# Attention in a fused Trainium2 kernel: bulk loads and the stores of x1 issued by ScalarE, and the inverse sums' way through memory as two items

## What is computed

```
q, k, v = split(x @ c_attn_w.T + b)              # 16 heads of 16
q_lat, k_lat, v_lat = q @ q2l, k @ kv2l, v @ kv2l  # 32 latents a head
q_lat, k_lat = rope(q_lat), rope(k_lat)
att = softmax(causal((q_lat @ wqk.T) @ k_lat.T * 32**-0.5))
y   = (att @ v_lat) @ l2o.T, heads joined, @ cproj.T
x1  = layernorm(x + y)
f   = layernorm(x1 + two_of_eight_experts(x1)) * g + b   # gate, top 2; w1, norm, gelu, w2
out = layernorm(x1 + f)
```

## Time and profile before

| | before |
|---|---|
| runs (us) | 2360.25, 2360.39, 2362.74; median 2360.39 |
| profiled execution: span | 2336.8 us; its total is not listed |
| attention phase, first x to the late items | about 27 to 1577 us of the span |
| expert and combining phases | about 1665 to 2337 us |
| TensorE / VectorE / ScalarE / GpSimd busy | 90% / 74% / 58% / 56% |
| granted TensorE clock, mean | 0.939 |
| SyncE's queue (q1) | 236.43 MB |
| ScalarE's queue (q10) | 9.44 MB |

### The profile page before, as it was taken

The page is one execution under the profiler, slowest core; times in us unless marked ns, Lnnn a source line. Parts: engine busy times, 40 slices in busy tenths (PEclk is TensorE's granted clock), DMA queues, the critical chain, the costliest instruction groups (busy, mean ns, idle before and its releaser), DMA issues. The chain is left out here.

```text
span 2336.8 us, 43530 instructions
## 1 busy us (share of the span) xinstructions
PE 2092.7 (90%) x12268; PEld 1464.7 (63%) x12268; DVE 1721.4 (74%) x4995; ACT 1365.5 (58%) x3316; POOL 1308.8 (56%) x1478
## 2 busy tenths in 40 slices
PE   4898999899899899899999999983399999999698
PEld 3554655555555555465556555642399999999587
DVE  3676687677678668668767767836488888888498
ACT  1265655655565565565555556563288887888454
POOL 2355464654764665666465476454577777777000
PEclk7899998999999999999889899995699999999899
DMA  6556556546565554655654556515122222222575
GB/s 176 127 135 142 118 115 149 126 106 150 127 135 128 135 122 118 156 118 116 149 123 109 140 124 146 115 39 213 26 74 74 76 75 76 74 74 69 182 243 168
DMA packets 190406, 284.46 MB, mean 122 GB/s; under 512 B 54072, under 2 KB 111056, under 8 KB 190032
## 3 DMA queue, kind: packets, MB, share of 16 engines
q1 hardware_dynamic: 168608, 236.43, 42.7%
q0 software_dynamic: 17152, 35.81, 5.0%
q10 hardware_dynamic: 4416, 9.44, 1.1%
HBM read 100.03 MB, written 37.90 MB: 59 GB/s over the span
## 5 line engine op out<-in xcount | busy, mean ns | idle before, releaser
L544 ACT ACTIVATE probs<-scores_T 128x512 f32<-128x512 f32 (+3 forms) x1536 | 654.4, 492 | 243.8 <-PE scores_T L433 240.7
L783 POOL TENSOR_SCALAR_AFFINE_SELECT probs<-probs 128x256 f32<-128x256 f32 x512 | 205.7, 410 | 522.4 <-ACT probs L544 519.4
L492 PE MATMUL ring<-k_stack,q_stack_b 96*128 96x512 f32 (+3 forms) x1024 | 396.3, 429 | 22.1 <-DVE neg_part L691 10.4
L691 DVE TENSOR_REDUCE neg_part<-ring 128x1 f32<-128x512 f32 x512 | 333.6, 685 | 97.6 <-PE ring L492 95.6
L433 PE MATMUL scores_T<-q_stack_b,k_stack 98*128 98x512 f32 (+3 forms) x1024 | 318.1, 387 | 45.4 <-ACT probs L544 44.5
L450 PE MATMUL o_ps<-probs,v_ones 128*17 128x512 f32 (+3 forms) x3072 | 341.8, 518 | 2.1 <-POOL probs L783 1.8
L492 PEld LDWEIGHTS ring<-k_stack,q_stack_b 96*128 96x128 f32 x1024 | 192.3, 196 | 227.4 <-issue 72.6
L696 DVE CUSTOM_DVE_ANT_0 ring<-ring,mask 128x384 f32<-128x384 f32 (+3 forms) x512 | 243.6, 508 | 113.5 <-PE ring L492 111.4
L696 DVE CUSTOM_DVE_ANT_0 ring<-ring,mask,neg_part 128x384 f32<-128x384 f32 (+3 forms) x512 | 260.5, 555 | 63.5 <-PE ring L492 63.3
L1107 ACT ACTIVATE o_sb<-ht_ps,ln_b,ln_g 128x128 f32<-128x128 f32 x544 | 217.9, 450 | 87.1 <-PE ht_ps L1056 86.6
L433 PEld LDWEIGHTS scores_T<-q_stack_b,k_stack 98*128 98x128 f32 x1024 | 186.3, 198 | 99.6 <-ACT probs L544 78.6
(11 more groups left out here) (190 smaller groups left out, 4552.8 us busy)
## 6 DMA issues: line engine op xcount, KB each, us to landing
u_rot<-u SPq DMA_DIRECT2D x128, 256.0 KB, 3.7
k_stack<-u_rot SPq DMA_DIRECT2D x128, 256.0 KB, 4.3
lat_w<-lat_split SPq DMA_DIRECT2D x32, 512.0 KB
q_stack_a<-u_rot SPq DMA_DIRECT2D x64, 256.0 KB
q_stack_b<-u_rot SPq DMA_DIRECT2D x64, 256.0 KB
k_stack<-u SPq DMA_DIRECT2D x64, 256.0 KB, 4.7
y<-y_rows SPq DMA_DIRECT2D x32, 512.0 KB, 6.7
x_raw<-in_xT SPq DMA_DIRECT2D x16, 512.0 KB, 5.3
```

Of the source, the lines that this page charges most:

```text
L492: nc.tensor.matmul(out[:, 0:k1 - k0], q_stack[qb // 4][0:3 * L, row_buf(n, qb // 4), h, P * (qb % 4):P * (qb % 4) + P], k_stack[0:3 * L, n ...
L544: nc.scalar.activation(probs[:, s % 2, h, cols], sc[(t + j) % 3][:, HALF - w:HALF], ACT.Exp).then_inc(exp_done, 1)
L691: nc.vector.tensor_reduce(neg_part[:, n % 2, part_col], src[:], AX_X, ALU.max, negate=True).then_inc(max_taken, 1)
L783: nc.gpsimd.affine_select(both, both, [[0, 2], [1, P]], ALU.is_ge, zero, base=0, channel_multiplier=-1).then_inc(kept, 1)
```

## The change

ScalarE's list now holds LAT, X, RES and the stores of x1 but the last one, and the loads and stores are issued there, with the waits they had (`bulk`). Every engine gets a list of its own from the same places plus a lag per engine and kind (`LAGS`); the only lag is -3.25 places for X on ScalarE. The places of X become (-58.75, 4.5), so that VectorE splits at 13.25 and 17.75 and ScalarE issues at 10 and 14.5. INV is cut into INV (7.25) and SPREAD (9.25), both SyncE's. A B item becomes two, one for each block, at the same place, so their order stays as it was.

```diff
--- before.py
+++ after.py
@@ -176,13 +176,16 @@
 
 
 PLACES = {
-    "LAT": (-53.5, 0), "Uq": (-50.25, 0.875), "SWAPq": (-49.25, 0), "ROPEq": (-45, 0), "WQ": (-41.5, 1.625),
+    "B": (0, 0),     "LAT": (-53.5, 0), "Uq": (-50.25, 0.875), "SWAPq": (-49.25, 0), "ROPEq": (-45, 0), "WQ": (-41.5, 1.625),
     "QL": (-41, 1.125), "STACKq": (-32.25, 0.875), "Uk": (-43.75, 0.625), "SWAPk": (-43, 0), "ROPEk": (-37.25, 0.5),
     "KH": (-34.75, 1.75), "KL": (-33.75, 1.875), "STACKk": (-29.75, 6.375), "S": (-27.75, 22.375), "MT": (-4.5, 0),
-    "MD": (-3.25, 0), "PV": (5.25, 2), "OE": (11.5, 15.625), "PACK": (24.75, 0), "RCP": (28.75, 0), "INV": (31.25, 0),
-    "Y": (36.5, 0), "X": (-60.75, 2.5), "V": (-23.5, 1.5), "RES": (4.5, 0), "ZB": (10.75, 0), "C": (39.5, 1),
+    "MD": (-3.25, 0), "PV": (5.25, 2), "OE": (11.5, 15.625), "PACK": (24.75, 0), "RCP": (28.75, 0), "INV": (31.25, 0), "SPREAD": (33.25, 0),
+    "Y": (36.5, 0), "X": (-58.75, 4.5), "V": (-23.5, 1.5), "RES": (4.5, 0), "ZB": (10.75, 0), "C": (39.5, 1),
     "NORM": (43.5, 0), "NX": (49.25, 0.75), "ZT": (53.5, 1.5), "G": (54.5, 1.5), "STORE": (68.25, 0),
     "R": (66.5, 0.375), "CNT": (72.25, 0.375), "SCAT": (77, 3.5)}
+
+
+LAGS = {"sync": {}, "tensor": {}, "scalar": {"X": -3.25}, "vector": {}, "gpsimd": {}}
 
 
 def attention_phase(nc, dram, wts, consts, xs, lat_dram, inv_dram, x1_dram, token_of_row, routes, tail, attention,
@@ -265,7 +268,7 @@
         def unit_items(n):
 
             b, g = n // GROUPS, n % GROUPS
-            at = [(HG * s + h, ("B", n, s, h)) for s in range(6) for h in range(HG)]
+            at = [(HG * s + h + j * PLACES["B"][1], ("B", n, s, h, j)) for s in range(6) for h in range(HG) for j in range(2)]
 
             def put(name, *items):
                 first, pace = PLACES[name]
@@ -290,6 +293,7 @@
             put("PACK", ("PACK", n))
             put("RCP", ("RCP", n))
             put("INV", ("INV", n))
+            put("SPREAD", ("SPREAD", n))
             if n % 2:
                 put("Y", ("Y", n))
             if g == 0 and b:
@@ -320,9 +324,16 @@
                     or it[0] in ("C", "NORM", "NX", "ZT", "G", "STORE", "R", "CNT", "SCAT") and it[1] == B - 1)
 
         R_STEPS, R_CHOSEN, R_COUNTED = 22, 12, 15
-        items = [it for _, it in sorted((p for n in range(UNITS) for p in unit_items(n)), key=lambda p: p[0])]
-        main, late = [it for it in items if not is_late(it)], [it for it in items if is_late(it)]
-        items = main + late
+        placed = [p for n in range(UNITS) for p in unit_items(n)]
+        late = [it for _, it in sorted(placed, key=lambda p: p[0]) if is_late(it)]
+
+        def order_of(engine):
+
+            lag = LAGS[engine]
+            return [it for _, it in sorted(placed, key=lambda p: p[0] + lag.get(p[1][0], 0)) if not is_late(it)]
+
+        main = {engine: order_of(engine) for engine in LAGS}
+        items = main["tensor"] + late
         RING = ("S", "U", "WQ", "MT", "C", "ZT", "G", "V", "CNT")
         ring_place = {it: i for i, it in enumerate(it for it in items if it[0] in RING)}
 
@@ -346,6 +357,26 @@
 
         ring_users = sorted(ring_place, key=lambda it: ring_place[it])
 
+        def bulk(engine, it):
+            kind, n = it[:2]
+            if kind == "LAT":
+                if n:
+                    engine.wait_ge(u_ready[1], 2 * n)
+                engine.dma_start(lat_w[:].bitcast(F32), lat_dram[n % GROUPS]).then_inc(lat_loaded, 16)
+            elif kind == "X":
+                kc = it[2]
+                if 2 * n + kc > KC:
+                    engine.wait_ge(x_lo_ready, 2 * n + kc - KC)
+                engine.dma_start(x_raw[:], dram["xT"][n, P * kc:P * kc + P, :]).then_inc(x_loaded, 16)
+            elif kind == "RES":
+                if n:
+                    engine.wait_ge(x1_stored, 16 * n)
+                    engine.wait_ge(logits_ready, TB * n)
+                engine.dma_start(z[:], dram["x"][n].rearrange("(tb p) c -> p tb c", p=P)).then_inc(res_loaded, 16)
+            elif kind == "STORE":
+                engine.wait_ge(x1_ready, TB * n + TB)
+                engine.dma_start(x1_dram[n].rearrange("(tb p) c -> p tb c", p=P), z[:]).then_inc(x1_stored, 16)
+
         def sync_items(sp, items):
             for it in items:
                 kind, n = it[:2]
@@ -353,15 +384,6 @@
                     for dst, name in ((rank, "rank"), (base, "base"), (before, "before"), (ones, "ones"),
                                       (ids_f, "ids_f")):
                         sp.dma_start(dst[:], dram[name]).then_inc(tables, 16)
-                elif kind == "LAT":
-                    if n:
-                        sp.wait_ge(u_ready[1], 2 * n)
-                    sp.dma_start(lat_w[:].bitcast(F32), lat_dram[n % GROUPS]).then_inc(lat_loaded, 16)
-                elif kind == "X":
-                    kc = it[2]
-                    if 2 * n + kc > KC:
-                        sp.wait_ge(x_lo_ready, 2 * n + kc - KC)
-                    sp.dma_start(x_raw[:], dram["xT"][n, P * kc:P * kc + P, :]).then_inc(x_loaded, 16)
                 elif kind == "SWAP":
                     s = it[2]
                     sp.wait_ge(u_ready[s], 2 * n + 2)
@@ -396,20 +418,15 @@
                 elif kind == "INV":
                     sp.wait_ge(inv_ready, n + 1)
                     sp.dma_start(inv_dram[n].rearrange("h (j i) -> (h j) i", i=L), inv[:]).then_inc(inv_kept, 16)
+                elif kind == "SPREAD":
                     sp.wait_ge(inv_kept, 16 * n + 16)
                     if n >= 2:
                         sp.wait_ge(y_ready, n // 2)
                     row = P // 2 * (n % 2)
                     sp.dma_start(inv_rep[row:row + P // 2, :],
                                  inv_dram[n].unsqueeze(1).to_broadcast([HG, HD, T])).then_inc(inv_spread, 16)
-                elif kind == "RES":
-                    if n:
-                        sp.wait_ge(x1_stored, 16 * n)
-                        sp.wait_ge(logits_ready, TB * n)
-                    sp.dma_start(z[:], dram["x"][n].rearrange("(tb p) c -> p tb c", p=P)).then_inc(res_loaded, 16)
-                elif kind == "STORE":
-                    sp.wait_ge(x1_ready, TB * n + TB)
-                    sp.dma_start(x1_dram[n].rearrange("(tb p) c -> p tb c", p=P), z[:]).then_inc(x1_stored, 16)
+                elif kind == "STORE" and n == B - 1:
+                    bulk(sp, it)
 
         def tensor_items(pe, items):
             for it in items:
@@ -420,19 +437,19 @@
                     if place >= 4:
                         pe.wait_ge(*freed(ring_users[place - 4]))
                 if kind == "B":
-                    s, h = it[2:]
-                    t = 2 * (24 * n + HG * s + h)
-                    if s == 0 and h == 0:
+                    s, h, j = it[2:]
+                    t = 2 * (24 * n + HG * s + h) + j
+                    if s == 0 and h == 0 and j == 0:
                         pe.wait_ge(max_row, 64 * n + 64)
                         if n == 0:
                             pe.wait_ge(consts_set, 3)
                     c, blocks = step_blocks(s)
-                    for j, (kb, q0, w, cols) in enumerate(blocks):
-                        if t + j >= 3:
-                            pe.wait_ge(exp_done, t + j - 2)
-                        nc.tensor.matmul(sc[(t + j) % 3][:, HALF - w:HALF], k_stack[:, n % 2, h, P * kb:P * kb + P],
-                                         q_stack[c][:, row_buf(n, c), h, q0 - HALF * c:q0 - HALF * c + w],
-                                         start=True, stop=True).then_inc(sc_full, 1)
+                    kb, q0, w, cols = blocks[j]
+                    if t >= 3:
+                        pe.wait_ge(exp_done, t - 2)
+                    nc.tensor.matmul(sc[t % 3][:, HALF - w:HALF], k_stack[:, n % 2, h, P * kb:P * kb + P],
+                                     q_stack[c][:, row_buf(n, c), h, q0 - HALF * c:q0 - HALF * c + w],
+                                     start=True, stop=True).then_inc(sc_full, 1)
                 elif kind == "PV":
                     s, j = it[2:]
                     b, g = n // GROUPS, n % GROUPS
@@ -534,15 +551,17 @@
                 if kind in RING:
                     place = ring_place[it]
                     src = ring[place % 4]
-                if kind == "B":
-                    s, h = it[2:]
-                    t = 2 * (24 * n + HG * s + h)
-                    if h == 0 and 6 * n + s >= 2:
+                if kind in ("LAT", "X", "RES") or kind == "STORE" and n < B - 1:
+                    bulk(act, it)
+                elif kind == "B":
+                    s, h, j = it[2:]
+                    t = 2 * (24 * n + HG * s + h) + j
+                    if h == 0 and j == 0 and 6 * n + s >= 2:
                         act.wait_ge(pv_done, 2 * (6 * n + s - 1))
-                    for j, (_, _, w, cols) in enumerate(step_blocks(s)[1]):
-                        act.wait_ge(sc_full, t + j + 1)
```

(22 more changed lines are left out.)

## The result

The kernel after takes **2379.59 us** (median of 9 runs, 2370.90 to 2386.96), beside 2360.25 for the kernel before in the same measurement (9 runs, 2351.24 to 2374.83). The ratio is **1.0071**, with an interval of 1.0044 to 1.0098: slower by 0.7%, where I forecast 0.3% faster. 2379.6 also lies above the range of 2334 to 2377. (Times here are medians over all runs of a kernel; the ratios leave out the few runs of before that a slower state of the chip disturbed.)

What follows compares the result with a forecast made beforehand. TensorE, busy 90% of the span, was taken as the bound through its standstills and half clock. Terms +3 + 2 + 5.6 - 14.0 - 2 - 1 = -6.4 us took 2360.4 to 2354 us; range 2334 to 2377.

Steps and rivals of the forecast that it cites:

- Who issues: SyncE's queue: losing 32 us of issues and sending q stacks sooner gains 0; bounds 0 and -9 us.
- First x: Early unit: VectorE's single 1.9 us wait for x goes away, -2 us; bounds 0 and -5.
- x's new places on VectorE: Splits at 13.25 and 17.75 don't fit before the transpose: +0.8 us in seven units, +5.6; bounds 0 and +16.
- the clock: TensorE in the six alike x units: all become the short 51.33 us kind, -14.0 us; bounds -25 and +14.
- ScalarE's issues: ScalarE carries 32 us of issues, 9% reaching TensorE: +3 us, or +8 if issues last 1.38 us; bounds 0 and +32.
- The wait moved to ScalarE: ScalarE, before x's second half: 1.2 us of wait less 0.9 idle, in seven units, +2 us; bounds 0 and +16.
- Latent weights later: Projection on TensorE: latent weights, issued later by ScalarE, still land in time, 0 us; bounds 0 and +24.
- Rival (c): Projection waits for latent weights if landing exceeds 4.3 us: +24 us, 2384 us; chance 0.12.
- The residual: GpSimd's 6.6 us of waits shrink as ScalarE issues the residual 1 or 2 us earlier: -1 us; bounds 0 and -6.6.
- The base: Whole kernel: profiled span 2336.8 us, with the median 23.6 us above it, left alone by the change.
- (b): Second split stops the transpose, half clock in all six x units: +14 and +3 us, 2377 us; chance 0.15.
- (a): Whole kernel: nothing moves, since SyncE had slack and ScalarE pays little; within 4 us of 2360; chance 0.25.

Runs made afterwards that it cites:

- experiment 9: Kernel after with all loads and stores issued by SyncE and x's splits at places 11.25 and 17.75: 2373.36 us, 1.0072 of before.
- experiment 7: Kernel after with only x on ScalarE (issues at 10 and 14.5); latent weights, residual and stores back on SyncE: 2374.88 us, 1.0046 of before.
- experiment 6: Kernel after with all loads and stores issued by SyncE, x at the new places (splits at 13.25 and 17.75): 2324.33 us, 0.9861 of before.
- experiment 12: Kernel after with everything issued by SyncE and x at its old places, only the cut items left: 2359.30 us, 0.9989 of before.
- experiment 10: Kernel after, all on SyncE, splits at 11.25 and 17.75, q stacks held until x's first half landed: 2350.19 us, 0.9971 of before.
- experiment 11: Kernel after with everything issued by SyncE and x's splits at places 13.25 and 15.75: 2338.54 us, 0.9920 of before.
- experiment 1: Kernel after with ScalarE issuing the first half of x at place 6.25 instead of 10: 2332.73 us, 0.9861 of before.
- experiment 5: Kernel after with x's first half issued at place 6.25 on ScalarE and the residual given back to SyncE: 2322.27 us, 0.9835 of before.
- experiment 8: Kernel after with only x on ScalarE, first half at place 6.25; latent weights, residual and stores on SyncE: 2323.07 us, 0.9856 of before.
- experiment 2: Kernel after with SyncE holding the q stacks in x units until x's first half is in: 2337.11 us, 0.9885 of before.

## Why the prediction was wrong

The order of issue against the clock of the unit explains the x units of all versions. Times are from the transfer of row maxima that opens the unit, each from one unit of the trace:

```
                          x issued   VectorE there   x landed    late by
before (from 1272.60)       24.3         31.7        by 31.7       -
all on SyncE, new places    24.1         35.2        by 35.2       -
experiment 9 (from 920.68)  24.1         31.7           34.4      2.7
after (from 914.27)         30.1         35.4           39.3      4.0
```

SyncE ran ahead of its list: with x at place 11.25 or 13.25 alike it issued the first half 24 us into the unit, as soon as the inverse sums had been spread. ScalarE, tied to its exps, reaches place 10 at 30 us. Beside the stacks the load takes 9 to 11 us; so it is just in time from 24 to 35 us, and 4 us late from 30.

Step by step:

- **Who issues** (0). SyncE's own time was indeed worth nothing, and the stacks did go out sooner. I named, SyncE standing for 10 us between x and the q stacks, and asked only who needed the stacks sooner. The question left out was who was served by their coming later: the first half of x. In that time it shared the DMA engines with the spreading of the inverse sums alone, issued 0.6 us ahead of it, and landed in 7.0 to 7.4 us.
- **No term for the first half's lead. This is the step that failed.** By my own places ScalarE issues at 10 and VectorE splits at 13.25: 3.25 places of 1.94 us are 6.3 us, already less than the longest landing of the earlier trace rows, 7.4. I never compared the two; I took those landings, measured with the q stacks held off, for granted and priced only *First x*, as a gain of 2. Measured: that term is a wait of 6.2 us where it was 1.9, with the early unit 3.3 us longer, and there are six more such waits. What it cost is experiment 7 against 6, 50 us (44 by the ratios), more than the upper bound of any of my terms.
- **x's new places on VectorE** (+5.6) **and the clock** (-14.0). The wait of the first term is there: with x in time TensorE stands 1.3 us ahead of the transpose in each x unit, where I had 0.8. The second was right in kind and too small: all six units are short, as I had taken them, but of 48.8 us rather than 51.33. In the profiled execution of experiment 6 they take 295.0 us against 322.0, -27.0, and the units behind them 5.7 more, so about -21 where my two terms make -8.4. I had read the half clock in the short units as belonging to the pause at place 11.25; it follows the second pause (experiment 12). By the ratio (0.9861) the whole of experiment 6 is worth -33 us. The reason I gave, that the first split came where VectorE had no gap, is what experiments 10 to 12 bear out for the pause; why the half clock behind it is long in some units stays open.
- **ScalarE's issues** (+3; bounds 0 and +32) cost nothing that shows. The issue takes 0.33 us on ScalarE, and TensorE's weight loads for scores waited on ScalarE 91.9 us in 140 waits against 94.7 in 144. The value of +8, by the rule of the Trainium skill's Perfetto Trace Analysis (DMA Instruction — HWDGE) about one issuer at a time, is not borne out: no ScalarE issue of latent weights took over 0.37 us. One of SyncE's issues of row maxima did take 2.58 us just behind ScalarE's store, but with everything on SyncE (experiment 6) one took 2.85.
- **The wait moved to ScalarE** (+2): 0. By my own numbers the wait was at most 0.9 us, not 1.2, and so no more than ScalarE's idle time. ScalarE comes to it 1.7 us after the first split has ended, because VectorE's wait for the first half has held up the exps too.
- **Latent weights later** (0, bounds 0 and +24): 2.2 us. TensorE waited for them 10.3 us in three waits, 8.1 of it for the first load, which before waited the same. Rival (c) falls.
- **The residual** (-1; bounds 0 and -6.6) has the wrong sign: +7.4 by the last unit of experiment 1 against 5, +11.2 by that of the change against experiment 7, +6 to +10.5 by the times. GpSimd's wait did fall, from 6.6 us to 2.0, as I wrote. I didn't ask what is under way when a 1 MB load starts: in the last unit the sums, 4.4 us of wait.
- **Stores, and the items cut in two** (0): experiments 5, 8 and 12 agree.
- **The base.** I took the profiled execution's span and the 23.6 us up to the median as a constant. In the runs since, only 1.8 us lie outside the span (2386.96 and 2385.2). If that held for it too, the profiled execution was itself some 22 us faster than the median; in one measurement 21 runs of before spread from 2333 to 2368. The interval of the ratio, 6.4 us either way, is also wider than the 4.7 us that I named as what a measurement can tell. The cut items with the old places show what a middling execution looks like: span 2354.4, with 325 us in the x units and 802.5 after the last unit, where the profiled execution of before has 322.0 and 793.6. What moves the late part I haven't tried.

By the ratios the parts are: cut items and new places -1.39% (experiment 6), x on ScalarE at place 10 +1.85% (experiment 7 less 6), and the residual with latent weights and stores +0.25% (1.0071 less experiment 7). Of 2360 us that is -33, +44 and +6, with intervals of 0.3 to 0.6% on each ratio, so the last part by itself is not clear of noise. (b) named a slower result near the true size, by another mechanism: with x in time a pause at the transpose is there (1.3 us in experiment 6), but the clock falls behind only three of the six, for 3.4 to 6.8 us and not for 17. (a), which the Trainium skill's DMA: Bandwidth & Descriptors (Issuing engines are not separate DMA queues) spoke for, fell on its time; yet the section as a whole agrees with the runs: by it transfers from all issuers run on the same 16 DMA engines and interleave, and x beside the stacks took 9.2 to 11.0 us from two queues and 9.7 to 10.5 from one. Read whole, it would have told me that x and the stacks, now on two queues, still travel together.

The best versions are experiments 5, 8, 6 and 1: 1.4 to 1.7% below before, not to be told apart from one another. Experiment 6 gets there with two numbers changed; the cut items that it keeps are worth nothing by experiment 12.

## What to carry to other kernels

When a queue stops at a wait, look at what is travelling meanwhile: the stop may be keeping other traffic off it, and taking the stop away makes that load late. For each moved load write down three times, its issue as the trace has it (not its place in a list), its landing with the traffic that will now be beside it, and its reader. A small transfer whose reader is near should not have a 1 MB load issued in the same microsecond.

## What the runs showed of the hardware

- 512 KB of x landed 3.4 to 3.6 us after its issue with no other issue beside it (x units of experiment 2), in 7.0 to 7.4 us when issued 0.6 us behind the spreading of the inverse sums (before), and in 9.2 to 11.0 with the six q stack copies beside it, whether these were issued just before it from another engine's queue (after) or just behind it on the same queue (experiment 9, 9.7 to 10.5).
- 16 KB of sums reached its reader 2.3 us after the issue, and 6.7 to 7.1 us after it when 1 MB was issued 0.04 to 0.06 us later from another queue (the last unit of five traces). With 1.4 us or more between the two, in the residual's other units of after, the reader wasn't held up.
- Pauses of TensorE of the same length were followed by very different stretches at 1.2 GHz. After 1.6 us at place 11.25: 17.1 us in two units of before, 20.5 in experiment 12 (the unit from 893.26), none in three units of experiment 10. After 1.3 us ahead of the transpose: none behind three of six in experiment 6, 3.4 to 6.8 us behind the other three. What tells them apart wasn't tried.
